# Attention keys laid out by head, a third stack buffer and an earlier copy schedule in a three-stage transformer kernel

## What is computed

```python
def _L0_xattn_ref(x, cond_k, cond_v, w_proj, b_proj):
    HEADS = 16
    d = W // H                      # 32
    scale = 1.0 / jnp.sqrt(jnp.sqrt(jnp.float32(d)))
    q = x.reshape(B, T, H, d) * scale          # B 4, T 128
    k = cond_k.reshape(B, S, H, d) * scale     # S 2048
    v = cond_v.reshape(B, S, H, d)
    scores = jnp.einsum('bthd,bshd->bhts', q, k)
    w = jax.nn.softmax(scores.astype(jnp.float32), axis=-1)
    out = jnp.einsum('bhts,bshd->bthd', w, v).reshape(B, T, W)
    return out @ w_proj.T + b_proj

x = x + _L0_xattn_ref(_layernorm(x), ctx_1024, ctx_1024, w_proj, b_proj)
x = x + _L0_attn_ref(_layernorm(x), ...)   # scan over the tokens
x = x + _L0_ffn_ref(_layernorm(x), ...)    # top 2 of 8 experts, and a shared part
```

## Time and profile before

| | us |
|---|---|
| runs | 536.25, 541.11, 542.07 |
| median of the three | 541.11 |
| profiled execution, device time | 539.15 |
| its span, first to last instruction | 537.4 |
| mean granted TensorE clock in it | 0.972 of full speed |

### The profile page before, as it was taken

How to read it: one execution, slowest core, us unless ns; L and a number is a source line. 1 busy time by engine, 2 the same in 40 slices (tenths; PEclk the granted TensorE clock), 3 DMA queues, 4 the chain that set the end, 5 groups by cost and what they waited for, 6 DMA issues and landing times.

```text
span 537.4 us, 15768 instructions
## 1 busy us (share of the span) xinstructions
PE 473.2 (88%) x6731; PEld 331.4 (62%) x6731; DVE 399.5 (74%) x603; ACT 330.2 (61%) x360; POOL 294.3 (55%) x278
## 2 busy tenths in 40 slices
PE   0579999798999898999989946997999999999995
PEld 0136667565666676666766533843788788887642
DVE  2686777477677677878762798788679999999426
ACT  3255867477567668776563463556478898887320
POOL 2358899699699999899769420472001011010032
PEclk9999999899899999999999995999999999999999
DMA  7798997959878879976696740228999999997135
GB/s 251 164 286 250 262 265 207 273 115 256 246 219 226 198 230 254 265 199 174 166 396 272 283 149 7 79 106 311 414 347 387 417 419 416 417 418 329 40 84 171
DMA packets 48249, 133.94 MB, mean 249 GB/s; under 512 B 6450, under 2 KB 31282, under 8 KB 37426
## 3 DMA queue, kind: packets, MB, share of 16 engines
q1 hardware_dynamic: 44500, 120.88, 69.6%
q0 software_dynamic: 3680, 12.06, 6.1%
HBM read 96.74 MB, written 11.01 MB: 201 GB/s over the span
## 4 chain that ended last, share of the span: by engine, by line
PE 45%; DVE 34%; issue 8%; DMA 7%; POOL 3%; ACT 1%; SPq 1%; DVEq 0%; ACTq 0%; POOLq 0%
DVE mx L696 12%; DVE ws L770 9%; PE bank L979 9%; PE bank L1014 8%; PE bank L1023 7%; PE bank L999 6%; DMA wst<-in_ffw 3%; DVE rden L713 2%; POOL xs_rows L660 2%; PE bank L1137 2%; PE bank L1139 2%; PE bank L1138 2%; DMA kt<-in_keysT 1%; DVE hf L908 1%; DMA x_tok<-xs_rows 1%
## 5 line engine op out<-in xcount | busy, mean ns | idle before, releaser
L696 DVE TENSOR_REDUCE mx<-bank 128x1 f32<-128x512 f32 x256 | 163.0, 685 | 67.9 <-PE bank L979 67.1
L457 ACT ACTIVATE pt<-bank 128x1024 f32<-128x1024 f32 x128 | 126.0, 1023 | 70.1 <-PE bank L999 70.1
L614 POOL TENSOR_TENSOR ps<-pt 128x512 f32<-128x512 f32 x128 | 160.0, 1277 | 10.1 <-ACT pt L457 5.2
L770 DVE SCALAR_TENSOR_TENSOR ws<-wst,ws 128x2048 f16<-128x2048 f32 x51 | 116.3, 2301 | 3.8 <-ACT ws L501 3.8
L979 PE MATMUL bank<-kstk,q 96*128 96x512 f16 x256 | 96.2, 407 | 24.9 <-DVE mx L696 8.1
L501 ACT ACTIVATE ws<-wst 128x2048 f16<-128x2048 f32 x48 | 90.4, 1904 | 7.1 <-DMA wst<-in_ffw 6.8
L999 PEld LDWEIGHTS bank<-q,kstk 98*128 98x128 f16 x1024 | 68.9, 100 | 22.5 <-issue 4.8
L587 POOL TENSOR_TENSOR kl<-kt,kh 128x512 f16<-128x512 f32 x62 | 70.6, 1162 | 22.3 <-ACT kh L422 22.3
L999 PE MATMUL bank<-q,kstk 98*128 98x128 f16 x1024 | 81.0, 224 | 1.0 <-ACT pt L457 1.0
L1152 PE MATMUL bank<-xt,ws 128*128 128x128 f16 x480 | 81.2, 219 | 0.6 <-DVE hf L908 0.6
L1153 PE MATMUL bank<-xt,ws 128*128 128x128 f16 x480 | 81.2, 219 | 0.0
(11 more groups left out here) (161 smaller groups left out, 639.0 us busy)
## 6 DMA issues: line engine op xcount, KB each, us to landing
wst<-in_ffw SPq DMA_DIRECT2D x51, 1024.0 KB, 10.8
kt<-in_keysT SPq DMA_DIRECT2D x16, 1024.0 KB, 6.0
kstk<-kh SPq DMA_DIRECT2D x128, 128.0 KB, 3.4
v<-in_vals SPq DMA_DIRECT2D x16, 1024.0 KB, 9.2
kstk<-kl SPq DMA_DIRECT2D x64, 128.0 KB, 3.7
xs_rows<-biases SPq DMA_DIRECT2D x15, 256.0 KB, 3.0
x_tok<-xs_rows POOLq DMA_DIRECT2D x15, 256.0 KB, 8.7
ys_rows<-xn POOLq DMA_DIRECT2D x15, 256.0 KB, 6.8
```

Source lines behind the costliest of these rows:

```text
L457: act.activation(pt[:, n % 4, :, :, :].rearrange("p j a t -> p (j a t)"), bank[:, 2 * (n % 2):2 * (n % 2) + 2, :].rearrange("p j n -> p (j ...
L614: pool.tensor_tensor(ps2[:, n % 4, :, :], pt[:, n % 4, 0, :, :], pt[:, n % 4, 1, :, :], ALU.add)\
L696: dve.tensor_reduce(mx[:, a, q:q + 1], bank[:, 4 + k % 2, :], AX.X, ALU.max).then_inc(m_taken, 1)
L770: dve.scalar_tensor_tensor(ws[:, home_of(q), 1, m, :, :].rearrange("p c n -> p (c n)"), wst[:, q % 2, m, :, :].rearrange("p c n -> p (c n) ...
```

## The change

Keys are laid out by head: `kt`, `kh` and `kl` hold head a on partitions 32a to 32a+31 with all 2048 positions in a row. `load_k` becomes four DMAs of 256 KB, one per head, each writing 32 partitions in pieces of 2 KB. The 12 copies of a group keep their size of 128 KB, read 32 partitions and write 32 as before, and move pieces of 4 KB; there is one semaphore per buffer and head. A third stack buffer lies in the second half of `wst`, so group j uses buffer j % 3; `stack(i+3)` stands in SP's list where `stack(i+2, ...)` stood, and the second three weight loads wait for the scores of group 14. The head is reordered: the rest of x waits for the first keys, head 0 of group 0 is copied before `load_k(1)`, the rows of ones are loaded behind the copies of group 0 (and a second time for the third buffer), ACT loads its tables with two small instructions ahead of need and splits groups 1 and 2 later, and the first 16 maxima go through six banks with one reduction of 128x1024 for two of them. PE computes the first two `scores` ahead of the first maxima of group 1.

```diff
-    kt = temp("kt", [P, 2, HG, S // 4], F32)
-    kh = temp("kh", [P, 2, HG, S // 4], F16)
-    kl = temp("kl", [P, 2, HG, S // 4], F16)
+    kt = temp("kt", [P, 2, S], F32)
+    kh = temp("kh", [P, 2, S], F16)
+    kl = temp("kl", [P, 2, S], F16)
     kstk = temp("kstk", [KM, 2, HG, S], F16)
+    third = wst[0:KM, 1, :, :, :].rearrange("p m c n -> p (m c n)").bitcast(F16)[:, 0:HG * S]
+    stacks = [kstk[:, 0, :, :], kstk[:, 1, :, :], third.rearrange("p (a s) -> p a s", a=HG)]
...
     def block_of(k):
-        h, k = divmod(k, 2 * HG)
-        return k // 2, 2 * h + k % 2
+        return divmod(k, S // 512)
...
         def load_k(j):
             if j >= 2:
                 sp.wait_ge(split_lo, j - 1)
-            sp.dma_start(kt[:, j % 2, :, :], t["keysT"][j]).then_inc(kt_in[j % 2], 16)
+            for a in range(HG):
+                sp.dma_start(kt[a * HD:(a + 1) * HD, j % 2, :].rearrange("d (q s) -> d q s", q=4),
+                             t["keysT"][j, :, a, :].rearrange("(q d) s -> d q s", q=4)).then_inc(kt_in[j % 2], 16)
...
-        def copies(j, h, src, rows):
-            for row in rows:
-                for q in (2 * h, 2 * h + 1):
-                    sp.dma_start(kstk[row:row + HD, j % 2, :, q * S // 4:(q + 1) * S // 4],
-                                 src[q * HD:(q + 1) * HD, j % 2, :, :]).then_inc(k_rep[j % 2][h], 16)
-
-        def stack(j, h):
+        def copy(j, a, src, row):
+            sp.dma_start(stacks[j % 3][row:row + HD, a, :], src[a * HD:(a + 1) * HD, j % 2, :])\
+                .then_inc(k_rep[j % 3][a], 16)
+
+        def stack(j):
             sp.wait_ge(split_lo, j + 1)
-            if j >= 2:
-                sp.wait_ge(st_done, HS * (j - 2) + HS // 2 * (h + 1))
-            copies(j, h, kh, (0, 2 * HD))
-            copies(j, h, kl, (HD,))
+            if j >= 3:
+                sp.wait_ge(st_done, HS * (j - 2))
+            for a in range(HG):
+                copy(j, a, kh, 0)
+                copy(j, a, kh, 2 * HD)
+                copy(j, a, kl, HD)

         sp.dma_start(x[:, 0, :], t["x"][:, 0, :]).then_inc(x0_in, 16)
         load_k(0)
         sp.dma_start(idh[:, :], t["idh"]).then_inc(id_in, 16)
-        sp.dma_start(kstk[KS:KM, :, :, :], t["ones"]).then_inc(id_in, 16)
+        sp.wait_ge(kt_in[0], 16 * HG)
         sp.dma_start(x[:, 1:B, :], t["x"][:, 1:B, :]).then_inc(x_in, 16)
+        sp.wait_ge(split_hi, 2)
+        copy(0, 0, kh, 0)
+        copy(0, 0, kh, 2 * HD)
+        sp.wait_ge(lo_dve, 2)
+        sp.wait_ge(split_lo, 1)
+        copy(0, 0, kl, HD)
         load_k(1)
-        sp.wait_ge(split_hi, 2)
-        copies(0, 0, kh, (0, 2 * HD))
-        sp.wait_ge(lo_dve, 1)
-        sp.wait_ge(split_lo, 1)
-        copies(0, 0, kl, (HD,))
-        stack(0, 1)
-        stack(1, 0)
+        for a in range(1, HG):
+            copy(0, a, kh, 0)
+            copy(0, a, kh, 2 * HD)
+            copy(0, a, kl, HD)
+        sp.dma_start(kstk[KS:KM, :, :, :], t["ones"]).then_inc(ones_in, 16)
+        sp.dma_start(stacks[2][KS:KM, :, :], t["ones"][:, 0, :, :]).then_inc(ones_in, 16)
         load_k(2)
         load_v(0)
-        stack(1, 1)
+        stack(1)
         load_k(3)
+        stack(2)
         for i in range(G):
...
-            if i + 2 < G:
-                stack(i + 2, 0)
-                stack(i + 2, 1)
+            if i + 3 < G:
+                stack(i + 3)
...
+        sp.wait_ge(st_done, HS * (G - 1))
+        for m in range(3):
+            sp.dma_start(wst[:, 1, m, :, :], t["ffw"][2, m]).then_inc(w_in[1][m], 16)
...
     def _(act):
...
+        act.wait_ge(eps_set, 2)
+        act.activation(r1[:, 0, 0:2], eps[:, :], ACT.Sqrt)
         for h in range(2):
             split_keys(0, h)
-        act.wait_ge(eps_set, 2)
         root(ln1_var, 1, 0, 1)
         queries_high(0)
         queries_high(1)
-        for h in range(2):
-            split_keys(1, h)
-        root(ln1_var, B, 1, B)
         take_queries(0)
         take_queries(1)
-        for h in range(2):
-            split_keys(2, h)
+        root(ln1_var, B, 1, B)
+        act.activation(r1[:, 1, 0:2], eps[:, :], ACT.Exp)
+        for j in range(1, 3):
+            for h in range(2):
+                split_keys(j, h)
         take_shifted(0)
...
     def _(dve):
...
-        for k in range(MB):
-            take_max(0, k)
+        for k in range(0, MB, 2):
+            a, q = block_of(k)
+            dve.wait_ge(m_ready, k + 2)
+            pair = 2 * (k // 2 % 3)
+            dve.tensor_reduce(mx[:, a, q:q + 2], bank[:, pair:pair + 2, :], AX.X, ALU.max).then_inc(m_taken, 2)
...
     def _(pe):
...
-            if k % (2 * HG) == 0:
-                pe.wait_ge(k_rep[j % 2][k // (2 * HG)], 16 * 6 * (j // 2 + 1))
-            if j > 0 or k >= 2:
+            if q == 0:
+                pe.wait_ge(k_rep[j % 3][a], 16 * 3 * (j // 3 + 1))
+            if j > 0:
                 pe.wait_ge(m_taken, MB * j + k - 1)
+            elif k >= 6 and k % 2 == 0:
+                pe.wait_ge(m_taken, k - 4)
+            home = 4 + k % 2 if j > 0 else k % 6
...
-        first_products(-1, 3)
+        pe.wait_ge(ones_in, 32)
+        scores(0)
+        scores(1)
+        for j, k in maxima_in(-1, 3):
+            max_scores(j, k)
```

More of the change, by code:

```diff
@@ L200, in build_program @@
     x0_in = sem("x_first_batch_loaded")
-    id_in = sem("identity_and_ones_loaded")
+    id_in = sem("identity_loaded")
+    ones_in = sem("ones_rows_loaded")
     kt_in = [sem("kt_loaded_0"), sem("kt_loaded_1")]
     v_in = [sem("v_loaded_0"), sem("v_loaded_1")]
-    k_rep = [[sem(f"k_stacked_{q}_{h}") for h in range(2)] for q in range(2)]
+    k_rep = [[sem(f"k_stacked_{q}_{a}") for a in range(HG)] for q in range(3)]
     split_hi = sem("split_hi")
@@ L374, in _ @@
             if i == G - 2:
-                for u in range(2):
-                    for m in range(3):
-                        sp.dma_start(wst[:, u, m, :, :], t["ffw"][2 * u, m]).then_inc(w_in[u][m], 16)
+                for m in range(3):
+                    sp.dma_start(wst[:, 0, m, :, :], t["ffw"][0, m]).then_inc(w_in[0][m], 16)
+        sp.wait_ge(st_done, HS * (G - 1))
+        for m in range(3):
+            sp.dma_start(wst[:, 1, m, :, :], t["ffw"][2, m]).then_inc(w_in[1][m], 16)
         sp.wait_ge(zero_set, 1)
@@ L415, in split_keys @@
         def split_keys(j, h):
-            heads = slice(h * HG // 2, (h + 1) * HG // 2)
+            part = slice(h * S // 2, (h + 1) * S // 2)
             if h == 0:
-                act.wait_ge(kt_in[j % 2], 16 * (j // 2 + 1))
+                act.wait_ge(kt_in[j % 2], 16 * HG * (j // 2 + 1))
                 if j >= 2:
-                    for half in range(2):
-                        act.wait_ge(k_rep[j % 2][half], 16 * 6 * (j // 2))
-            act.activation(kh[:, j % 2, heads, :].rearrange("p a s -> p (a s)"),
-                           kt[:, j % 2, heads, :].rearrange("p a s -> p (a s)"), ACT.Copy).then_inc(split_hi, 1)
+                    for a in range(HG):
+                        act.wait_ge(k_rep[(j - 2) % 3][a], 16 * 3 * ((j - 2) // 3 + 1))
+            act.activation(kh[:, j % 2, part], kt[:, j % 2, part], ACT.Copy).then_inc(split_hi, 1)
         def root(ready, count, b0, b1):
@@ L599, in queries_low @@
             pool.tensor_tensor(z[:, :, 2 * HD:KS], q, z[:, :, 0:HD], ALU.subtract).then_inc(xs_lo, 1)
-        for a in range(2, HG):
-            split_keys(0, a)
+        split_keys(0, 3)
         queries_low(0)
@@ L605, in _ @@
         for j in range(1, 3):
-            for a in range(HG):
-                split_keys(j, a)
+            for c in range(4):
+                split_keys(j, c)
         queries_low(2)
@@ L731, in _ @@
         first_norm(0, 1)
-        dve.wait_ge(split_hi, 1)
-        dve.tensor_tensor(kl[:, 0, 0:2, :], kt[:, 0, 0:2, :], kh[:, 0, 0:2, :], ALU.subtract).then_inc(lo_dve, 1)
+        for h, part in ((0, slice(0, 1024)), (1, slice(1024, 1536))):
+            dve.wait_ge(split_hi, h + 1)
+            dve.tensor_tensor(kl[:, 0, part], kt[:, 0, part], kh[:, 0, part], ALU.subtract).then_inc(lo_dve, 1)
         dve.wait_ge(roots, 1)
```

21 lines of the change are left out of this document (11 added, 10 removed).

## The result

The kernel after runs in 546.76 us (median of 4, 545.72 to 551.34), the kernel before in 541.59 (median of 4, 536.25 to 542.27) beside it. The ratio on record is 1.016, with an interval of 1.011 to 1.021; the two medians alone give 1.010. It is slower by about 1 to 2%, where 537.0 and a small gain were forecast. The profiled execution after took 545.78 us, with a span of 544.0 against 537.4.

A forecast was written before the change was run, and what follows sets the result against it. POOL's beat of 15.19 us per group was taken as the bound, with 11.4 us lost to late copies. Head +4.3, stalls -11.4 and queue +3 gave 4.1 us less, 537.0 us; range of 8 in 10: 523 to 551.

The forecast's parts named there:

- The stalls of the kernel before: Attention: 11.4 us lost to late copies over 12 intervals, all removed by issuing copies one group ahead.
- rival C: Attention: a late key load, not late copies, starts the stalls, so they stay; +4.3 us, 545; chance 0.1.
- What bounds a group: Attention: POOL's beat, with PE right beside it, keeps 15.19 us as the floor of a group.
- The rate of the key loads: DMA queue: loads onto 32 partitions run at 202 GB/s, 5.2 us per group, because of the partitions, not the pieces.
- Rival A: DMA queue: key loads to 32 partitions run at full rate and all stalls go; -13.4 us, 527.7; chance 0.2.
- The queue's price: Attention: 15.55 us of queue per group against a beat of 15.19 costs 3 us, bounds 0 and 13.
- SP itself has room: Attention: SP's 17 issues of about 0.65 us take 11 us of 15.2.
- The head: Start of the kernel up to group 0's inversion: it comes at 62.5 against 58.20, 4.3 us later.
- part of these 7.4 us comes back: Head: ACT's later keys 3 cost 7.4 us, partly regained as PE and POOL go ahead, leaving 4.3 us.
- keys 3 decide: Head: keys 3, landing at 50 against 42.63, set when group 0 ends, since keys 2 land earlier, about 35.
- the 4 us for the ones: Head: the load of the rows of ones takes 4 us of the queue's 45.5 us sum.
- B: Attention: the queue becomes the bound, losing from 15.8 us of transfers per group; 550 at 16.4; chance 0.2.

The follow-up runs named there:

- e3: The kernel before with only the third stack buffer and the copies one group further ahead; 533.52 us, ratio 0.989.
- e12: The kernel after with one key load onto all partitions and ones by memset, but copies held back as two buffers would hold them; 568.49 us, ratio 1.054.
- e13: The kernel after with the values loaded ahead of the keys in SP's list; 541.4 us, ratio 1.001.
- e9: The kernel after with its four key loads in 2 KB pieces each going onto all 128 partitions; 540.01 us, ratio 0.998.
- e14: The kernel after with one key load per group onto all 128 partitions, in 2 KB pieces; 534.66 us, ratio 0.990.
- e1: The kernel after with keys by head in HBM already, in one 1 MB load onto all partitions in 8 KB pieces; 534.22 us, ratio 0.990.
- the square above: Four kernels: after (546.76 us), with one key load onto all partitions (534.22), with ones by memset (544.01), with both (529.22).
- e4: The kernel after with the ones loaded ahead of the rest of x; 545.94 us, ratio 0.999.

## Why the prediction was wrong, point by point

By its own terms, on the profiled executions: the forecast was +4.3 for the head, -11.4 for the stalls and +3 for the queue, -4.1 in all. Measured: +8.6, and -0.3 for both others together, -1.7 in the rest, +6.6 in all. The miss of 10.7 us is 4.3 in the head and 8.1 in the queue, less 1.7. Two steps failed: the 3 us for the queue, and in the head the time that was to come back together with the price of the ones.

**The stalls of the kernel before: right.** They are late copies, and the lead takes them all: e3 wins 11.1 of the 11.4 in the 12 intervals, e12 loses them again. This rules out rival C.

**What bounds a group: right, with 0.08 us missing.** All kernels with the new layout have 15.26 or 15.27, those with the old 15.19. PE's waits per group, four for two, are one of the things that differ, but no run tests that; it is 1 us over 12 groups.

**The rate of the key loads: right.** 32 partitions decide, not the size of pieces: 213 GB/s for a share of 1 where 202 was taken, about 10 us of the time for 32 partitions and nothing seen for the pieces. Rival A falls with it.

**The queue's price: the step that failed most.** It says: "values and keys have a few us in hand before they are waited for, so I take 3 us". Of 12 undisturbed intervals (183.2) the kernel after is 10.2 us away, near the upper bound of 13. I had priced the mean excess of the queue over the beat, 15.55 against 15.19. That excess isn't there: a share of 0.92 over groups of 16.1 us is 14.8 us of the queue per group, and the sign of 0.95 or more between 60 and 240 us didn't come. What costs is that single loads come late although the queue has room on the mean. For the values of group 1 this is shown, by the wait of 3.0 us and by e13. Their landing times in general grew little (10.0 us from issue to landing, 9.2 before), as these rows of after show:

```profile
kt<-in_keysT SPq DMA_DIRECT2D x64, 256.0 KB, 5.5
v<-in_vals SPq DMA_DIRECT2D x16, 1024.0 KB, 10.0
```

The values are loaded one group ahead, as before, and nothing in the change lengthens that. Of the 10.2 us, by the profiles, 6.1 are the 32 partitions (after against e9), 2.2 the number of DMAs (e9 against e14), and 1.9 are in e14 and not in e1. That late values are what turns them into time in every group is argued, beyond group 1. The other part of the failure is the number of DMAs, which "SP itself has room" priced at nothing. Four loads for one cost about 4 us in the new order and over 20 in the old one. By which mechanism stays open: e9 has the share of e14, its values land as fast (8.8 and 9.1 us), only its last copies land later (`wst<-kl` 4.3 against 3.0), and no run separates the issue on SP from what the DMA engines do with more transfers.

**The head: its landings about right, its end wrong.** Keys 0 landed at 9.31 (forecast 9 to 10), the first maxima began at 16.24 (15), the last were taken at 31.09 (29), keys 2 came at 35.63 (35), keys 3 at 52.30 (50), and the doubled reduction took 1.15 to 1.18 us (1.25):

```profile
17.38 2.35 DVE L755 TENSOR_REDUCE mx<-bank 128x2 f32<-128x1024 f32 x2 [0.89 <-PE bank L997]
24.21 6.88 DVE L755 TENSOR_REDUCE mx<-bank 128x2 f32<-128x1024 f32 x6 [4.47 <-PE bank L997]
```

The step that failed is "part of these 7.4 us comes back, since PE and POOL go ahead in the meantime". Keys 3 were 9.7 us later than in the kernel before (52.30 against 42.63), and 8.6 of them stand in the head's end. In the forecast's terms, 2.3 of the 4.3 us missing are keys 3 (52.30 for 50), and 2.0 are what didn't come back: from keys 3 to the inversion it took 14.5 us, where 12.5 was forecast and 15.6 was the time before.

Nor do "keys 3 decide" alone. ACT waited for them 1.68 us, not 7. By then it was late already: its third exponent began at 47.29, after 5.75 us of waiting for PE, and at 38.36 in the kernel before. PE had started late since keys 2 came at 35.63, and then stood 2.31 us, until 42.43, before the first maxima of group 1. The trace names no releaser there; by the code it is the copies of group 1. Keys 2, these copies and keys 3 stand in one queue and were late together, so no engine could work ahead.

And the 4 us for the ones were about the load's own time (in after its records take 2.2 us for 32 KB and 1.2 for 16 KB), but not its effect: without it the head is 6.5 us shorter. The key loads, put down with 4 x 2.6 us, were worth 2.2 to 3.3 in the head (the square above), and moved keys 3 by 2.8 (52.30 to 49.51 in e1). That the sum came within 2.3 us of keys 3 is luck in part: one term was too small and the other too large.

**The rivals.** B, the queue as the bound and the kernel slower, came true: at 0.2 it had too small a chance. It named 15.8 us of transfers per group as its point; after has groups of 193.38 / 12 = 16.1 us on the mean, but 14.8 us of transfers in them, so the queue is not the bound that B describes. It priced 550 against 546.8 measured. Its sign was wrong: there is no wait of ACT on keys in the groups of after; it showed only in e13, where the values went first. The measured ratio, 1.016, lies in the range and not where most of the chance was.

**The rest at nothing: right, as far as it can be seen.** The three weight loads that were moved and the stages behind the attention took 1.7 us less, within what the other kernels have there.

## What to carry to other kernels

A lead of one more buffer removes waits only while the queue behind it has room, and room is not the mean share: look at which load is issued last in each burst, and how long it takes from issue to use. When a layout makes one load into several, or lets it write a quarter of the partitions, price both, and try the new buffer alone before the layout: here the buffer alone was worth 1.1% and, with constants written by an idle engine instead of loaded, 3.1%. In a head that hangs on one queue, don't count on work of other engines going ahead, and put the load that the first exponent waits for first. And when a part of the profile behind the change moves by a few us, compare it over all kernels before you explain it.

## What the runs showed of the hardware that was not expected

- Loads of 96 KB in all onto two partitions put the end of the head off by 6.5 to 8.3 us in three kernels; 64 KB put it off by 1.2 in the kernel before. In after the loads left two records of 32 KB (2.2 us each) and two of 16 KB (1.2 us), in e1 of 2.8 to 3.1 and 2.0 us. The Trainium skill ("DMA: Bandwidth & Descriptors", the section on why a DMA increments its semaphore by 16) says that a transfer issued from SyncE uses the largest number of engines, 16 at most, that divides the outermost dimension on both sides; that is two here, and the two records per load agree. Why it costs more than its own time stays open; e4, which moved it, was too unsteady to say.
- A 2 KB piece of a key load took 151 ns when the load went onto 32 partitions and 84 ns when it went onto all 128 (medians, after against e9 and e14).
- Four loads for one, with the same bytes, pieces and partitions, cost about 4 us over 16 groups at an unchanged share of 0.84.
- A memset of 2x4096 in single precision took DVE 3.47 us, hidden in the head.
